# A causal linear attention's products on all four quadrants of the array, instead of the two on its diagonal

## The reference, cut to what matters

```python
phi_q = relu(q) + 0.001;  phi_k = relu(k) + 0.001          # [B, S, H=16, DH=16]
kv  = cumsum_s(einsum('bshm,bshd->bshmd', phi_k, v))
num = einsum('bshm,bshmd->bshd', phi_q, kv)
den = einsum('bshm,bshm->bsh', phi_q, cumsum_s(phi_k))
attn = num / den[..., None]
```

## Time and profile before

| | before |
|---|---|
| device time, median of 3 | 2015.1 us |
| time of the profiled execution | 2020.32 us |
| its span | 2018.5 us |
| PE busy | 1890.2 us, 94% |
| PE weight loads (PEld) busy | 1595.4 us, 79% |
| DVE busy | 1596.6 us, 79% |
| ScalarE (ACT) busy | 514.7 us, 25% |
| GpSimd (POOL) busy | 231.8 us, 11% |

### The profile page before, as it was taken

One profiled execution on the slowest core, in us unless ns is written; L12 is line 12 of the kernel. 1 busy time (PEld: TensorE's weight loads), 2 busy tenths in 40 slices (PEclk: granted clock), 3 DMA queues, 4 the chain that ended last, 5 costly groups with the idle time before them and its releaser, 6 DMA issues. The chain is left out here.

```text
span 2018.5 us, 58331 instructions
## 1 busy us (share of the span) xinstructions
PE 1890.2 (94%) x18240; PEld 1595.4 (79%) x18240; DVE 1596.6 (79%) x6197; ACT 514.7 (25%) x1120; POOL 231.8 (11%) x514
## 2 busy tenths in 40 slices
PE   6775688999999999999999999999999999999997
PEld 3443477888888888888888888888888888888886
DVE  4557887888888888888888888888888888887432
ACT  4341012222221313232222222131323222222222
POOL 0001101011010102020101111110202010110100
PEclk9885598999999999999999999999999999999998
DMA  6852010100010010101010001000010101010000
GB/s 233 270 149 55 13 28 14 29 20 24 15 33 14 21 27 14 29 18 29 20 28 20 24 16 31 14 23 25 17 30 16 29 20 28 20 29 8 1 7 6
DMA packets 100871, 72.98 MB, mean 36 GB/s; under 512 B 64744, under 2 KB 94448, under 8 KB 99568
## 3 DMA queue, kind: packets, MB, share of 16 engines
q1 hardware_dynamic: 98272, 67.54, 11.6%
q10 hardware_dynamic: 2320, 1.85, 0.3%
HBM read 45.74 MB, written 23.59 MB: 34 GB/s over the span
## 5 line engine op out<-in xcount | busy, mean ns | idle before, releaser
L1557 DVE CUSTOM_DVE_ANT_0 state<-decayed_state,bank 128x128 f32<-128x128 f32 x2048 | 507.2, 287 | 83.0 <-PE bank L1094 72.0
L1547 DVE TENSOR_TENSOR decayed_state<-state,decay 128x128 f32<-128x128 f32 x2048 | 517.8, 293 | 9.0 <-issue 6.8
L1193 PE MATMUL bank<-f_w_sb,hs_whole 128*128 128x256 f32 x2048 | 489.0, 382 | 0.0
L1193 PEld LDWEIGHTS bank<-f_w_sb,hs_whole 128*128 128x128 f32 x2048 | 373.9, 190 | 49.8 <-ACT hs_whole L987 5.3
L987 ACT ACTIVATE hs_whole<-bank,f_b_sb 128x256 f32<-128x256 f32 x512 | 214.1, 469 | 695.7 <-PE bank L1180 695.6
L1094 PE MATMUL bank<-xrows,brows 128*128 128x256 f32 x1024 | 261.1, 345 | 44.5 <-DVE state L1557 33.0
L1094 PEld LDWEIGHTS bank<-xrows,brows 128*128 128x128 f32 x1024 | 175.2, 199 | 94.9 <-issue 56.0
L1180 PE MATMUL bank<-late_fT_parts,f_w_hi 128*128 128x256 f32 x1024 | 179.3, 298 | 0.5 <-ACT hs_whole L987 0.5
L1180 PE MATMUL bank<-fT_parts,f_w_hi 128*128 128x256 f32 x1024 | 166.7, 288 | 0.0
L1180 PEld LDWEIGHTS bank<-late_fT_parts,f_w_hi 128*128 128x128 f32 x1024 | 143.8, 192 | 15.6 <-issue 11.5
L1675 DVE SCALAR_TENSOR_TENSOR x<-bank,comb,x 128x256 f32<-128x256 f32 x256 | 111.8, 479 | 52.3 <-PE bank L1193 50.6
(11 more groups left out here) (155 smaller groups left out, 2420.6 us busy)
## 6 DMA issues: line engine op xcount, KB each, us to landing
brows<-bs_dram SPq DMA_DIRECT2D x1020, 2.0 KB
xrows<-xs_dram SPq DMA_DIRECT2D x480, 32.0 KB
xt<-in_x SPq DMA_DIRECT2D x4, 1024.0 KB, 7.8
xn_dram<-xn SPq DMA_DIRECT2D x4, 1024.0 KB, 5.4
z_dram<-zT SPq DMA_DIRECT2D x4, 1024.0 KB, 4.1
f_w_sb<-in_f_w SPq DMA_DIRECT2D x2, 2048.0 KB
xs_dram<-xhi SPq DMA_DIRECT2D x4, 1024.0 KB, 5.2
xs_dram<-xlo SPq DMA_DIRECT2D x4, 1024.0 KB, 8.4
```

What stands on the lines that cost most here:

```text
L1193: last = pe.matmul(bank_[:, tile * D:(tile + 1) * D], hs_whole[:, slot, m, tile * P:(tile + 1) * P], w(m), start=(m == 0 and tile == 0 and ...
L1547: dve.tensor_tensor(decayed_state[:, part], state[:, (s - 1) % RING, part], decay[:, part], ALU.mult).then_inc(decayed.sem, 1)
L1557: dve._custom_dve(add_sat, out=state[:, s % RING, part], in0=decayed_state[:, part], in1=U[s // 2 % 2][:, s % 2 * D + h * HALF:s % 2 * D + ...
```

## The change

`ACROSS = GH // 2 = 2`. Of the four head slots hh = 0 to 3 of each group of heads, slots 0 and 1 still write to the partitions of their batch; slots 2 and 3 write to the other half. For this

- `from_chunk` goes through pairs of slots (hh and hh + 2), so that four products in a row lie on quadrants (0, 0), (64, 64), (0, 64) and (64, 0); their number stays 32 in each call.
- `from_states` splits each product of 68 columns into two of 34, one for each half of PSUM: 32 products instead of 16.
- `attended` multiplies slots 0 and 1 of a tile in one instruction on 128 partitions, and slots 2 and 3 in two on 64 partitions each, which bring the result back to the partitions of its batch: 6 multiplications instead of 2.
- `from_chunk(0)` now signals, and PE waits for that signal ahead of `from_chunk(1)`; without it two halves of the array's rows could write the same bank at once.
- `at_done` counts 6 instead of 2, `num_made` counts 2 instead of 1.

```diff
-                def tpose_set(c, k, done, dst=TB):
+                def tpose_set(c, k, done, dst=TB, n_done=TILES):
...
+                def placed(bb, across):
+                    half = 1 - bb if across else bb
+                    return slice(CT * half, CT * (half + 1)), CT * half
+
                 def from_states():
-                    W = GH * HV
+                    W = ACROSS * HV
...
-                                pe.matmul(NB[tile][CT * bb:CT * (bb + 1), gr * W:(gr + 1) * W], qT[:, gr, b * CT:(b + 1) * CT],
-                                          kv[:, bb, tile, gr * W:(gr + 1) * W], start=(gr == 0), stop=False, skip_group_check=True)
+                                for across in range(2):
+                                    at = gr * GH * HV + across * W
+                                    pe.matmul(NB[tile][placed(bb, across)[0], at:at + W], qT[:, gr, b * CT:(b + 1) * CT],
+                                              kv[:, bb, tile, at:at + W], start=(gr == 0 and bb == 0), stop=False, skip_group_check=True)
 
                 def from_chunk(crossed):
-                    for hh in range(GH):
+                    for pair in range(GH // 2):
                         for gr in range(GROUPS):
-                            hd = gr * GH + hh
-                            for tile in range(TILES):
-                                bb = (tile + crossed) % 2
-                                part = slice(CT * bb, CT * (bb + 1))
-                                last = pe.matmul(NB[tile][part, hd * HV:(hd + 1) * HV], ss[part, hh, tile * GROUPS + gr, :], vv[part, tile, hd, :],
-                                                 start=False, stop=(hh == GH - 1), skip_group_check=True, tile_position=(CT * bb, CT * bb))
+                            for across in range(2):
+                                hh = ACROSS * across + pair
+                                hd = gr * GH + hh
+                                for tile in range(TILES):
+                                    bb = (tile + crossed) % 2
+                                    part = slice(CT * bb, CT * (bb + 1))
+                                    rows_, column = placed(bb, across)
+                                    last = pe.matmul(NB[tile][rows_, hd * HV:(hd + 1) * HV], ss[part, hh, tile * GROUPS + gr, :], vv[part, tile, hd, :],
+                                                     start=False, stop=(pair == GH // 2 - 1), skip_group_check=True, tile_position=(CT * bb, column))
...
-                from_chunk(0)
+                from_chunk(0).then_inc(num_made.sem, 1)
                 u(27)
                 y(5)
+                wait_apart(num_made, num_made.after(c, 1))
                 from_chunk(1).then_inc(num_made.sem, 1)
                 first_layer(late, 1, 6)
-                tpose_set(c, T_WO, at_done, HB[1])
+                tpose_set(c, T_WO, at_done, HB[1], 3 * TILES)
...
                     for tile in range(TILES):
                         dve.wait_ge(rec_done.sem, rec_done.after(c, tile + 1))
-                        dve.tensor_tensor(turn[:, tile].rearrange("p (h m) -> p h m", h=H), nums[tile][:, :, 0:DH],
-                                          rec[:, tile].unsqueeze(2).broadcast_to([P, H, DH]), ALU.mult).then_inc(at_done.sem, 1)
+                        at = turn[:, tile].rearrange("p (g h m) -> p g h m", g=GROUPS, h=GH)
+                        by = rec[:, tile].rearrange("p (g h) -> p g h", g=GROUPS)
+                        for across in range(2):
+                            slots = slice(ACROSS * across, ACROSS * (across + 1))
+                            for to, of in ((slice(0, P), slice(0, P)),) if not across else ((slice(0, CT), slice(CT, P)), (slice(CT, P), slice(0, CT))):
+                                dve.tensor_tensor(at[to, :, slots, :], nums[tile][of, :, slots, 0:DH],
+                                                  by[of, :, slots].unsqueeze(3).broadcast_to([of.stop - of.start, GROUPS, ACROSS, DH]),
+                                                  ALU.mult).then_inc(at_done.sem, 1)
```

More of the change, by code:

```diff
@@ L598, in main_part @@
         MASK_ORDER = (3, 0, 1, 2)
+        ACROSS = GH // 2
         LATE_HIDDEN = (0, 1, 0, 0, 0, 0, 0, 0)
@@ L655, in main_part @@
         rec_done = signal("rec_done", TILES)
-        at_done = signal("at_done", TILES)
+        at_done = signal("at_done", 3 * TILES)
         xr_done = signal("xr_done", 1)
@@ L675, in main_part @@
         scored = signal("scored", 1)
-        num_made = signal("num_made", 1)
+        num_made = signal("num_made", 2)
         kv_half = signal("kv_half", 1)
@@ L1129, in transposes @@
                     return last
-                def tpose_set(c, k, done, dst=TB):
+                def tpose_set(c, k, done, dst=TB, n_done=TILES):
                     if c is None:
                         return
-                    pe.wait_ge(done.sem, done.after(c, TILES))
+                    pe.wait_ge(done.sem, done.after(c, n_done))
                     transposes(late_turn if k in (T_MLP, T_FFN2) else turn, dst).then_inc(tposed[k].sem, 1)
@@ L1719, in attended @@
                         return
-                    dve.wait_ge(num_made.sem, num_made.after(c, 1))
-                    nums = [bs[:, 0:H * HV].rearrange("p (h v) -> p h v", h=H) for bs in NB]
+                    dve.wait_ge(num_made.sem, num_made.after(c, 2))
+                    nums = [bs[:, 0:H * HV].rearrange("p (g h v) -> p g h v", g=GROUPS, h=GH) for bs in NB]
                     for tile in range(TILES):
-                        dve.reciprocal(rec[:, tile], nums[tile][:, :, DH]).then_inc(rec_done.sem, 1)
+                        dve.reciprocal(rec[:, tile], nums[tile][:, :, :, DH].rearrange("p g h -> p (g h)")).then_inc(rec_done.sem, 1)
                     for tile in range(TILES):
                         dve.wait_ge(rec_done.sem, rec_done.after(c, tile + 1))
-                        dve.tensor_tensor(turn[:, tile].rearrange("p (h m) -> p h m", h=H), nums[tile][:, :, 0:DH],
-                                          rec[:, tile].unsqueeze(2).broadcast_to([P, H, DH]), ALU.mult).then_inc(at_done.sem, 1)
+                        at = turn[:, tile].rearrange("p (g h m) -> p g h m", g=GROUPS, h=GH)
[6 more added lines that the diff above has]
+                                                  ALU.mult).then_inc(at_done.sem, 1)
                 def add_states():
```

## The result

| | before | after |
|---|---|---|
| median, us (14 runs each, taken in turn) | 2018.05 | 2025.24 |
| range, us | 2010.89 to 2025.02 | 2020.60 to 2030.81 |
| ratio to before, 95% interval | | 1.0035 (1.0022 to 1.0049) |
| profiled execution: time, span, us | 2020.32, 2018.5 | 2024.16, 2022.1 |

The changed kernel is slower by 0.35%, 7.2 us by the medians; +3.9 us was forecast. Applied to the 2015.1 us that the prediction starts from, that is 2022.2 us; 2019.0 was forecast.

The account below looks back on a forecast made before the run. PE was taken to set the pace of the full steps, with DVE late next. Full steps +9.1, chunk 0 -2.7, chunk 15 -2.5 sum to +3.9 us: 2019.0 us against the 2015.1 median, range 2009 to 2034.

Parts of the forecast that it names:

- Step 1: from_chunk on four quadrants: weight loads 14.4 ns apart instead of 28.7, each call 0.92 us shorter.
- Step 2: from_states with 64 instructions instead of 32: half width is no cheaper, adding 0.92 us that nothing hides.
- Step 3: attended's six multiplications start 0.21 us apart; the last ends 1.62 us after the first reciprocal starts, instead of 1.05.
- Step 4: T_WO waits for DVE's last multiplication: 1.5 us of PE stall, and a gain of 0.27 us there.
- Behind T_WO: After T_WO in a full step: PE and DVE both go on as now.
- +0.65 a step: Each of 14 full steps lengthens by +0.92 from from_states less 0.27 at T_WO, in all +9.1 us.
- The ends: Chunks 0 and 15 gain from shorter from_chunk calls: -2.7 us and -2.5 us.
- No overlap: Rival: quadrants sharing rows don't load together, from_chunk stays as it was; about +19 us, 2034 us; chance 0.08.
- half price: Rival: half-width products make from_states cost nothing more, T_WO still gains 0.27 us; about 2006 us; chance 0.12.
- Dearer pieces: Rival: from_states' half order blocks (+1.8 us) or multiplications take 0.32 us each; 2028 to 2031 us; chance 0.20.
- The clock: Rival: stall and low-width products take the grant to 1.2 GHz in full steps; +31 us, 2050 us; chance 0.06.

Follow-up runs that it names:

- e1: Kernel before with from_states alone split into 32 products of 34 columns instead of 16 of 68; ratio to before 1.0024.
- e3: Kernel before with attended's two multiplications cut into four of 8 heads each, all on 128 partitions; 2013.2 us in one run.
- e6: Changed kernel with its six multiplications reordered: both on 128 partitions first, then upper half to lower, then lower to upper; ratio to before 0.9995.
- e2: Changed kernel with the two old multiplications, rows not brought back, so the result is not the reference's; ratio to before 0.9938.
- e7: Kernel before with 32 empty PE instructions written into each step ahead of T_WO, most likely never there; ratio to before 0.9986.
- e4: Kernel before with attended's two multiplications cut into four by pairs of slots, all on 128 partitions; 2018.6 us in one run.
- e5: Kernel before with each multiplication cut into three (128 partitions, lower 64, upper 64), nothing crossing halves; 2018.4 us in one run.
- e8: Kernel before with 32 empty PE instructions written once ahead of the chunk loop, most likely never there; ratio to before 1.0011.
- e9: Changed kernel with quadrants dealt by head groups instead of slots, from_states back at 16 products of 68 columns; ratio to before 1.0290.
- e11: e10 with new_states(0) moved ahead of T_WO, into PE's wait for the multiplications; ratio to before 1.0194.
- e10: e9 with two multiplications again, rows brought back by the T_WO transposes through an identity with swapped halves; ratio to before 1.0197.
- e12: e10 with 16 products of new_states(0) issued twice per step, first ahead of T_WO; ratio to before 0.9882.

## Why the prediction was right where it was, and wrong where it was

**Step 1, right.** The 64 weight loads of from_chunk went from 1.94 to 1.02 us: -0.92, as forecast, and (1.02 - 0.135) / 63 = 14.0 ns apart. Quadrants that share rows do load together: 14.0 ns is half of the 28.7 of two quadrants.

**Step 2, right.** 1.03 to 1.95 us: +0.92. e1 shows it alone, +0.90 at `T_WO`. Half the columns cost as much as all of them.

**Step 3, wrong in size.** "So I take 0.21": it is 0.32. The last multiplication ends 2.17 us after the first reciprocal starts, not 1.62. The range named 0.32, but for a wrong reason (a strided operand); e3 to e6 show that it is the change of start partition. The row that I took the 0.21 from is a run of instructions that all start at partition 0. This is the term that was mis-sized, by +0.55 us.

**Step 4, right as a mechanism, its 1.5 us by luck.** `T_WO` waits for DVE, with 1.44 us of idle before its weight loads (1.5 forecast). But DVE is done 0.55 us later than forecast, so PE, on the path that I gave it, would have waited some 2 us. from_chunk(1) was not done "1.84 us sooner": 0.7 us of the time saved went into the wait of `u(27)` for DVE's scan, which I had taken as 1.4 us of mere work. That miss costs nothing, since `T_WO` waits behind it. Waits of the changed kernel over 11 steps (us, times, longest):

```profile
PEld bank L1128 <- DVE turn L1743: 15.8, 11, 1.5
PE bank L1128 <- DVE turn L1743: 13.6, 11, 1.3
```

`T_WO` moved by +1.21 where +0.65 was forecast; step 3's 0.55 is the difference.

**Behind T_WO, wrong.** "both go on from there as now": they did not. 0.62 us came back, 0.48 of it because the longer loop no longer has the stall at its head. So the +0.65 a step that stood in the sum, and the +0.59 measured, agree by two misses of one size and opposite sign. Had the stall stayed, a step would have been 0.59 + 0.48 = 1.07 us longer, and the kernel some 6 us slower than it is; this counterfactual is worked out, no run shows it. e6 and e2 likewise owe 6 us of their gain to it.

**The ends, right by luck.** I forecast -2.7 for chunk 0 and -2.5 for chunk 15, and the executions show -3.6 and -2.9. But the kernel before ran these stretches at a lower clock in its profiled execution, and that was what I priced. Stretches of 12 us from chunk 0's from_states and of 10 to 12 from chunk 15's on (PE busy, PEld, DVE, ACT, POOL, granted clock third last), before:

```profile
306.50:319.00 12.50, 10.52 (x181) 8.60 (x182) 8.70 (x39) 0.00 (x0) 0.00 (x0) 0.65 0.10 26
1939.00:1951.00 12.00, 11.61 (x197) 10.61 (x200) 2.93 (x8) 0.91 (x3) 0.00 (x0) 0.76 0.01 3
```

The changed kernel:

```profile
306.70:319.00 12.30, 8.72 (x285) 7.38 (x286) 11.29 (x51) 0.60 (x1) 0.00 (x0) 0.93 0.11 28
1946.00:1956.00 10.00, 9.08 (x281) 7.99 (x281) 3.44 (x11) 1.18 (x4) 0.00 (x0) 1.00 0.01 3
```

And e7, whose instructions stand in the order of before:

```profile
301.40:313.80 12.40, 10.45 (x253) 9.04 (x254) 10.41 (x48) 0.60 (x1) 0.00 (x0) 0.85 0.09 26
1933.00:1943.00 10.00, 9.89 (x249) 9.04 (x250) 2.54 (x8) 1.50 (x5) 0.00 (x0) 1.00 0.02 3
```

In e7 `T_WO` comes 9.03 us (chunk 0) and 8.28 us (chunk 15) behind from_states, in the changed kernel at 9.70 and 8.64: later, not 2.5 us earlier. And e1, without the faster from_chunk, needs 109.55 and 75.98 us for the two parts where the changed kernel needs 109.61 and 76.12. So nothing shows that the four quadrants bring anything at the ends. (e7 needs 111.95 and 74.08. From chunk 0 to 1 PE runs 17.1 us at 1.2 GHz in the execution of before, 13.7 in e7, and 6.8 in e1 and the changed kernel. What sets that, no run shows.) The timed medians say the same: they differ by 7.2 us, close to the 7.7 of the full steps alone; without the -5.2 us of the ends the forecast would have been +9.1. The +2.3 us from chunk 14 to 15 are the clock too: 6.8 us at 1.2 GHz, where the executions of before and e7 have none (102.06 and 102.23 us). But e3, e4, e5 and e8, all in before's order, also have 6.8 us there and need 105.4 to 106.1 us, so the change is not needed for it.

**The rivals.** No overlap fell with step 1 (14.0 ns, above 24 would have decided for it), half price with step 2. "Dearer pieces" was half true: the multiplications at 0.32 us, but the order of from_states does not block. The clock held 1.00 in the full steps of the changed kernel, and in e9 to e11 it fell only at the branch and behind it. Half price was priced at about 2006 us, and its terms give 2005. That the cost of the multiplications and the code's layout would pull in opposite directions was in no case of mine.

## What to carry to other kernels

Count the DVE instructions that start at other partitions than their predecessor, and order them so that like stands by like: here it took 0.37 us off the path (11.28 to 10.91), and the loss was no longer to be seen. A transpose that runs anyway brings rows back across partitions for nothing, where multiplications on half the partitions cost 1.15 us a step. When a kernel with a long loop gets slower or faster for no reason in its waits, look at the branch's own duration and at the count of instruction pieces before believing the story: with two PE instructions more a step came out 3.3 us longer, and with another 64 it was 4.4 us shorter.

## What the runs showed of the hardware that was not expected

- Consecutive multiplications of 128 elements per partition on DVE start 0.20 to 0.22 us apart when they start at the same partitions and 0.30 to 0.32 when not, whatever the number of partitions.
- PE can stand still 3.65 us at a loop's branch with every input ready. The branch then lasts 3.0 to 3.9 us instead of 0.36 and ends 1.30 to 1.53 us after a piece of 16 KB of instructions has landed, in 39 of 39 passes (e9, e10, e11); one piece more per pass is fetched (143 instead of 130 in 13 steps), and the granted clock over the next 4 us is 0.66 (e10). Which lengths or places of the loop bring this about, no run shows: 2353 and 2354 instructions do, 2351, 2415, 2417 and 2418 don't.
- A second stall of 0.24 to 0.92 us, at `mlp_second(0)` about 2.8 us behind the same branch, appears in all runs whose loop has before's length (before, e3, e4, e5, e7, e8) and in none of e1, e2, e6, e12 and the changed kernel. Like the first, it ends 1.2 to 1.6 us after a piece has landed, in 78 of 78 steps.
- A transpose by TensorE with a permuted identity permutes the result, at the transposes' usual pace: from the first weight load of `T_WO` to the next group's it is 0.39 us in e10 and in the changed kernel.
